# Two-layer decoder on one core: the layer norm's epsilon in the statistics, shorter gate weights, one rounding step, and a new instruction order

## The reference, cut to what matters

```python
def _layernorm(x, axis=-1, eps=1e-05):
    m = jnp.mean(x, axis=axis, keepdims=True)
    v = jnp.var(x, axis=axis, keepdims=True)
    return (x - m) / jnp.sqrt(v + eps)
...
    # _L0_ffn_ref
    a_scale = jnp.max(jnp.abs(x), axis=-1, keepdims=True) + EPS
    z = jnp.clip(x / a_scale * 127.0, -128.0, 127.0)
    a_quant = z + jax.lax.stop_gradient(jnp.round(z) - z)
...
    # _L1_ffn_ref
    gate_logits = jax.nn.softmax(x @ gate_w + gate_b, axis=-1)
    selected = (gate_logits >= THRESHOLD).astype(x.dtype)
    weights = gate_logits * selected
    wsum = jnp.sum(weights, axis=-1, keepdims=True)
    weights = weights / jnp.where(wsum == 0, jnp.ones_like(wsum), wsum)
```

## Time and profile before

| what | value |
|---|---|
| time, median of 3 runs | 508.68 us (508.4 to 509.6) |
| span of the profiled execution | 507.0 us |
| PE busy | 492.5 us, 97% |
| PEld busy | 417.4 us, 82% |
| ACT busy | 438.2 us, 86% |
| DVE busy | 411.2 us, 81% |
| POOL busy | 390.3 us, 77% |
| DMA, mean over the span | 17 GB/s |

### The profile page before, as it was taken

How to read it: one execution, slowest core, us unless ns; L and a number is a source line. 1 busy time by engine, 2 the same in 40 slices (tenths; PEclk the granted TensorE clock), 3 DMA queues, 4 the chain that set the end, 5 groups by cost and what they waited for, 6 DMA issues and landing times.

```text
span 507.0 us, 15965 instructions
## 1 busy us (share of the span) xinstructions
PE 492.5 (97%) x5508; PEld 417.4 (82%) x5508; DVE 411.2 (81%) x939; ACT 438.2 (86%) x1177; POOL 390.3 (77%) x553
## 2 busy tenths in 40 slices
PE   6999999999999999999999999999999999999994
PEld 3878887788888888889888888888988888888882
DVE  3867787887989888989898898888888788876665
ACT  4988889999999888998899998999889899898761
POOL 3787678787678689897798877988777788685663
PEclk8999999999999999999999999999999999999998
DMA  6800000000000000000000000000000000000000
GB/s 197 324 3 2 1 3 1 3 3 2 1 3 1 8 2 8 1 7 3 7 3 7 2 2 8 2 6 3 8 6 2 7 1 5 6 1 8 1 6 16
DMA packets 6462, 8.65 MB, mean 17 GB/s; under 512 B 1393, under 2 KB 4849, under 8 KB 6385
## 3 DMA queue, kind: packets, MB, share of 16 engines
q1 hardware_dynamic: 5952, 6.86, 4.1%
q10 hardware_dynamic: 432, 0.79, 0.5%
HBM read 6.50 MB, written 1.05 MB: 15 GB/s over the span
## 4 chain that ended last, share of the span: by engine, by line
PE 76%; DVE 9%; ACT 6%; issue 3%; DVEq 3%; POOL 1%; DMA 1%; POOLq 0%; SPq 0%; ACTq 0%
PE psum L1188 11%; PE psum L1215 8%; PE psum L1243 8%; PE psum L1175 8%; PE psum L1131 7%; PE psum L1162 5%; ACT w_cross L776 3%; PE psum L1201 2%; PE psum L1360 2%; PE psum L1254 2%; PE psum L1234 2%; PE psum L1226 2%; PE psum L1228 2%; PE psum L1227 2%; PE psum L1236 2%
## 5 line engine op out<-in xcount | busy, mean ns | idle before, releaser
L694 POOL TENSOR_TENSOR w_self<-w_self 128x1024 f16<-128x1024 f32 x64 | 120.9, 1899 | 13.8 <-ACT w_self L759 9.9
L776 ACT ACTIVATE w_cross<-psum,row_max_cross 128x128 f32<-128x128 f32 x384 | 104.5, 405 | 6.8 <-DVE row_max_cross L922 6.2
L699 POOL TENSOR_TENSOR w_cross<-w_cross,e_rec_cross 128x1024 f32<-128x1024 f32 x48 | 91.0, 1899 | 10.3 <-DVE e_rec_cross L931 9.7
L922 DVE TENSOR_REDUCE row_max_cross<-psum 128x8 f32<-128x1024 f32 x48 | 58.0, 1214 | 9.9 <-PE psum L1175 9.5
L929 DVE TENSOR_REDUCE e_sum_cross<-w_cross 128x8 f32<-128x1024 f32 x48 | 58.3, 1215 | 1.8 <-ACT w_cross L776 1.7
L1175 PE MATMUL psum<-kT_cross,qT_cross 64*128 64x128 f32 x768 | 54.2, 283 | 0.0
L1215 PEld LDWEIGHTS psum<-w_cross,v_cross 128*64 128x64 f32 x768 | 41.2, 136 | 15.3 <-issue 13.0
L784 ACT ACTIVATE w_cross<-psum 128x1024 f32<-128x1024 f32 x48 | 50.0, 1048 | 3.2 <-PE psum L1188 3.2
L1215 PE MATMUL psum<-w_cross,v_cross 128*64 128x128 f32 x768 | 51.4, 278 | 0.9 <-ACT w_cross L784 0.6
L1175 PEld LDWEIGHTS psum<-kT_cross,qT_cross 64*128 64x128 f32 x768 | 46.2, 187 | 6.9 <-issue 4.8
L1188 PE MATMUL psum<-ident,w_cross 128*128 128x128 f32 x384 | 49.5, 274 | 0.8 <-POOL w_cross L699 0.8
(11 more groups left out here) (198 smaller groups left out, 1412.5 us busy)
## 6 DMA issues: line engine op xcount, KB each, us to landing
out_dram<-x_all SPq DMA_DIRECT2D x16, 64.0 KB, 1.5
x_all<-in_x SPq DMA_DIRECT2D x1, 768.0 KB, 7.0
cT_all<-in_ctx SPq DMA_DIRECT2D x1, 768.0 KB, 9.0
e_k<-in_e_k SPq DMA_DIRECT2D x1, 512.0 KB, 4.7
e_v<-in_e_v SPq DMA_DIRECT2D x1, 512.0 KB, 5.6
e_q<-in_e_q SPq DMA_DIRECT2D x1, 512.0 KB, 8.9
e_o<-in_e_o SPq DMA_DIRECT2D x1, 512.0 KB, 9.7
m_w<-in_m_w SPq DMA_DIRECT2D x1, 512.0 KB, 9.0
```

What stands on the lines that cost most here:

```text
L694: pool.tensor_tensor(L.w_low[u], L.w[u][:], halves(L.w[u][:]), ALU.subtract)\
L699: pool.tensor_tensor(L.diff[u][:].rearrange("p (h k) -> p h k", h=UNIT), L.e[u][:].rearrange("p (h k) -> p h k", h=UNIT), L.e_rec[:, u, :] ...
L776: last = act.activation(L.e[u][:, P * p:P * (p + 1)], S_[:, P * p:P * (p + 1)], ACT.Exp, bias=L.row_max[:, u, p:p + 1])
L922: dve.tensor_reduce(L.row_max[:, u, :], group(i, turn)[:].rearrange("p (h k) -> p h k", h=UNIT), AX_X, ALU.max, negate=True).then_inc(L.ma ...
```

## The change

- The statistics get a third group of three numbers (count 0, mean 0, sum of squares 128 times epsilon), written once at the start for each of the six stages. The aggregate over nine numbers then gives variance plus epsilon, and the addition on POOL goes.
- `gate_weights` compares the unscaled exponentials with a tenth of their sum, takes the masked product and its sum in one instruction, and divides by that sum. The first reciprocal, one of the two scaled copies and the guard go; a copy of the exponentials to SBUF and a multiplication of one column come.
- `round_units` no longer clips ahead of the rounding.
- The planner's costs for `rs`, `ffn.xTe` and `moe.w` are lowered, and so is its cost of a change of tiling ahead of `pv` in cross attention. The strings of PE, DVE, ACT and POOL are new. SP's is the same.

```diff
-        add(f"{L}.rs", "POOL", 1272, [source], [f"{L}.nm"])
+        add(f"{L}.rs", "POOL", 940, [source], [f"{L}.nm"])
...
-    add("moe.w", "DVE", 1650, ["moe.ex"], ["moe.ml", "moe.gT"])
+    add("moe.w", "DVE", 1240, ["moe.ex"], ["moe.ml", "moe.gT"])
...
 ORDER = dict(
     ACT=(
-        "aGaqaIasaKauaMaGa7a5a5awa5aIa5aRa7a7aVaKaybXbXbXaGaAbZb3a7bZa0b3aIaGaMaVbZbZaRa7aKaCb1b1b1a9bbaMaIbd"
+        "aqaGasaIaKa5aMaua5a5aGa5a7awaIaRa7aKa7aVaybXbZbXaAa7bZb1aGb3bZbZaMaVa0aIaRb1aKb1b1bXa9b3aGbba5a7bdaM"
...
 def switch(name):
     step = name.split(".")[1]
-    return 150 if step in ("xT", "oT", "gT", "t") else 107 if step == "pv" and name[:4] == "self" else 196
+    if step == "pv":
+        return 107 if name[:4] == "self" else 147
+    return 150 if step in ("xT", "oT", "gT", "t") else 196
...
-        self.moments = self.sb("moments", [P, 6])
+        self.moments = self.sb("moments", [P, 9])
         self.mean_var = self.sb("mean_var", [P, 2])
-        self.var_eps = self.sb("var_eps", [P, 1])
...
-                pool.tensor_tensor(L.var_eps[:], L.mean_var[:, 1:2], eps[:], ALU.add)
-                pool.drain()
-                pool.tensor_tensor(L.rstd[:], L.var_eps[:], minus_half[:], ALU.pow)
+                pool.tensor_tensor(L.rstd[:], L.mean_var[:, 1:2], minus_half[:], ALU.pow)
...
-                dve.tensor_scalar(units, units, Q_MAX, -Q_MAX - 1, ALU.min, ALU.max)
+
                 if i:
                     dve.wait_ge(x_full, full(i - 1, "ffn.y"))
-                dve.drain()
...
                 dve.wait_ge(gate_exp, i + 1)
-                dve.reciprocal(g_rec[:], g_sum[:])
-                dve.drain()
-                dve.tensor_scalar(g_soft[:], gates(i, 1), g_rec[:], None, ALU.mult)
-                dve.tensor_scalar(gates(i, 2), gates(i, 1), g_rec[:], None, ALU.mult)
-                dve.drain()
-                dve.scalar_tensor_tensor(out=gates(i, 3), in0=gates(i, 2), scalar=THRESHOLD, in1=g_soft[:],
+                dve.tensor_copy(g_exp[:], gates(i, 1))
+                dve.tensor_scalar(g_least[:], g_sum[:], THRESHOLD, None, ALU.mult)
+                dve.drain()
+                dve.scalar_tensor_tensor(out=gates(i, 2), in0=gates(i, 1), scalar=g_least[:], in1=g_exp[:],
                                          op0=ALU.is_ge, op1=ALU.mult, accum_out=g_keptsum[:])
                 dve.drain()
-                dve.tensor_scalar(g_guarded[:], g_keptsum[:], 0.0, g_keptsum[:], ALU.is_equal, ALU.add)
-                dve.drain()
-                dve.reciprocal(g_rec2[:], g_guarded[:])
+                dve.reciprocal(g_rec[:], g_keptsum[:])
...
+            for L in stages.values():
+                dve.memset(L.moments[:, 6:8], 0.0)
+                dve.memset(L.moments[:, 8:9], P * LN_EPS)
             dve.memset(g_weight[:], 0.0).then_inc(consts, 1)
```

More of the change, by code:

```diff
@@ L80, in norm @@
         fill(f"{L}.xT", 109, [f"{L}.un" if L == "ffn" else f"{L}.nm"], f"{L}.{read}", users)
-        add(f"{L}.xTe", *(("DVE", 572) if L == "ffn" else ("ACT", 332 if L == "moe" else 166)), [f"{L}.xT"])
+        add(f"{L}.xTe", *(("DVE", 250) if L == "ffn" else ("ACT", 332 if L == "moe" else 166)), [f"{L}.xT"])
     def self_attention(L, source, maxima, following, loads, loads_out):
@@ new lines @@
+        "beaUb0b2a4a1a6a4aXaObabWbjbcaLaUblaHaZaQaJa1bebnbWaXbWaLbYaHaOaZbwa4a1a4bab2bcbybjaUbeblbCaQaJbabEbn"
+        "bGbYaXbcbJaZaLb2bja1bebwbla6bya4a6aHbQaObCa6bEbna6baaUbSbGbjbcbUaQbJblb6bebwb8bybnccb0aXaJcabQbCaLbE"
+        "claZbGaHbSa1bUchbjbJcjblb6bwcqb8bacabyccclbncsbQaOa4b2bcbWbCaQbSbEcubUaJchaUbwa6bWbybeb6cqcaaXbJcsaZ"
+        "b8aLbGaHcya1clcccja4cBcCcubjbQb2aObCaJcGblbSa4baaUcya6bcbEbUbncBaQchbeb6bGcCbJaXcacKb8cGcqaLbwclcjcs"
+        "ccbQaZbycubWbSaHa1bYbjbUaOblbaaJbYbcbCaUcybnbEaQcqcBbGbWcKcCchb6bebJcscjbwcab8bycGaXclccaZa4aLa1bQcu"
@@ new lines @@
+        "bjaHa6aObCaJb0blbSbEaQbGbUbncybaaUcqcBcKbcchbJcsbeaXb6cCcaaZbwb8aLa1aHbyclcjccbQcGb2bWcubScKbjbUbCaO"
+        "blbab0bEbncyaQbcaJaUcBcCb6cqb8bGbebJcsaXchbwcaaLaZcccjcGbycla6a1cubjbQaHa4aOblbaaJa4bnaQbSbccybCaUbU"
+        "cKbEcBchcCcqbebJcscjaXb6bWaLb8aHbwaZcaa1bGbyccclcGcubjbYbQaOblbCbSb2bEbUbaaQbccybncKchb6aUcBb8bGcabe"
+        "bJcjbYcqcCccclcsaXcGbwcuaLbybjaJaZbQb0b0a1blaOaHbCbnbSbEa6a6aQbGcyaJbYcKbUcBaUbacCbcchcqb6bwbebJaXca"
+        "b8aLbycGcjcsccaZaHcla1cubjbYb0aOblbQb2bnbaaUbccyaQcKbSchcBaJcqbeaXbUcCcjcsaOb6b0aZb8bCcabEbGaLaQa1cc"
@@ new lines @@
+        "aYcmcda2bRcocvcfaPaTbocAbVcDaEcLcFbubKbNbfaYcIbxbha2cmbzcdbRcocvcLcfbVaPaTcAbocDcFcIbubfbNbKaYbhaEbx"
+        "cdbzcma2cfcvcobRaPaTbocAbVcDcLaEcFcIbubfbNbKaYbhbxa2aEcdbzcmcvcfbRaPbVaTcAcobocDcFcLbfbKbNbhcIbucdcm"
+        "bxaYcvbzcfbRa2coaPboaTcLcAbVcDbucFcIbxbfbNbKaYbhbzcdcma2cvcfcoaTaPbRbocAcDcLcFbfbVaYcIbhaPaTbua2cdbx"
+        "cmbzcfcvaYcobKbNboa2cAcDbfcLcFbhbRcIbubVbNbfcLbKcvbxbhcdbzcmbRcAbocfcDcocFbVcIbobubKbNbxbzcmcdbucvbR"
+        "cfcobxcAbVcDcLcFcIbzbNbKcdcmcvcfbRbKbVcobNcAcDcFcmbRcdbVcocfcLcIcvcdcAcmcLcfcocDcFcvcIcAcDcFcvcLcIcA"
@@ new lines @@
+        "aIaRaKaGaVa0bga5b1a5a9b3a7aCbbbXbkbdaMaVbmaIa0aRaKaGbgbXbtaIaMbZbvbXa0a9a5aGa5bbb3bda9bkbBaVbmbDaRbg"
+        "bbbHbFbZbtbdaKaMbva0bLbkbOb3bga7aIa9a7bBa5bmbDa7bFa7bbbTaVbHbkbdbtaRaGb5bvbmb7bLbOb9bgbBb1cecbbDaKbF"
+        "a0bHbTaMaIcncibtbkb5a9bvckb7bObmb9bbcbbLcrcecnctbtbBb3a5bdbDbXaRbvbTaGbFaKciaVb5a7bXb7crbgcbcxcta0bL"
+        "bHb9czaMbOaIcncka5cEcebkbBb3a9bDcHaKbTcxbmbba5aVcza7bFbdcEaRb5cibtb7bHbgbvaGbLcbb9bOcHcrckctcna0aMce"
+        "bXbTaIbZbkcxa9bBbmbbaKb5bDbZaVczbdbFaRcEaGbXbHcrbtb7cibvbgbOctcbb9cHbLcka0cncea5aMaIbBbka9cxa7bDaKb1"
@@ L545, in decoder @@
         g_rec = sb("g_rec", [P, 1])
-        g_soft = sb("g_soft", [P, EXPERTS])
+        g_exp = sb("g_exp", [P, EXPERTS])
+        g_least = sb("g_least", [P, 1])
         g_keptsum = sb("g_keptsum", [P, 1])
-        g_guarded = sb("g_guarded", [P, 1])
-        g_rec2 = sb("g_rec2", [P, 1])
         g_weight = sb("g_weight", [P, P])
@@ L890, in stats @@
                     dve.wait_ge(L.rstd_ready, i)
-                dve.bn_stats(L.moments[:], x)
+                dve.bn_stats(L.moments[:, 0:6], x)
                 dve.drain()
```

64 lines of the change are left out of this document (22 added, 42 removed).

## The result

The changed kernel takes 504.94 us (median of 5 runs, 504.84 to 506.29); the kernel before took 508.8 beside it (5 runs, 508.4 to 510.17). The ratio is 0.9928, with a 95% interval of 0.991 to 0.9947: faster by 0.7%, 3.9 us. The profiled execution's own time is 504.84, its span 503.1.

A forecast was written before the change was run, and what follows sets the result against it. PE was taken as the bound, its products busy for 97% of the 507.0 us span. Gains of 1.35 (start), 0.87 (end) and 0.7 (ramps), together 2.92, plus 1.68 from span to median gave 505.8 us, range 503.9 to 508.6.

The forecast's parts named there:

- the case of a faster kernel: Whole kernel: a mean below 507.15 us, given a chance of 0.71.
- Part 1: Norms on POOL: 0.34 us less each, 32.6 in all; nothing in the dense middle, full at start and last `moe`.
- The Trainium skill's warning: From 200 to 450 us, PE's busy products hide waits the new order removes: 3.3 us more, 502.5; chance 0.04.
- Part 2: Start: PE's first filler `cross0.k.0(0)` moves from 8.82 to 7.45, a gain of 1.35 us; twelve memsets cost 0.
- the lead of the start is lost: Waits come later, before 50 us, so the start's gain goes: 507.6 us, no change that can be told; chance 0.22.
- the rival with the clock: Below 20 us, PE works without a gap and keeps full clock: about 1.5 us more, 504.3; chance 0.14.
- Part 3: Clip on DVE, dense middle and ramps: some 0.35 us less per sequence, 5.6 in all, taken as worth 0.
- Part 4: Last `moe`: gate weights 0.53 us shorter plus the last norm's 0.34, so 0.87 gained after the last `cross1.y`.
- a sign of being wrong: At the end: a weighing on DVE that waits for POOL's mix of sequence 14 would show the forecast wrong.
- Part 5: Ramps: shorter chains arrive late less often, recovering 0.7 of PE's 3.92 us idle in ramps and middle.
- The rival of new waits: From 200 to 450 us, PE steps stand ahead of their inputs: 510.6 us at 0.3 us per sequence; chance 0.10.

The follow-up runs named there:

- experiment 7: Changed kernel with the old norm statistics (six numbers, addition of epsilon back on POOL): 514.78 us, ratio 1.011 to the kernel before.
- experiment 1: Kernel before with all code edits but its old planner costs and old order: 507.17 us, ratio 0.9955 to the kernel before.
- Experiment 10: Kernel before with seven unneeded PE products at its start and, of the change, only the statistics' third group: 506.81 us, ratio 0.9946.
- experiment 4: Changed kernel with DVE's low part of the context's first four sequences waiting for the first rstd: 506.6 us, ratio 0.9941 to the kernel before.
- experiment 3: Kernel before with seven unneeded PE products at its start, nothing else moved: 507.59 us, ratio 0.9967 to the kernel before.
- experiment 11: Changed kernel with the clip ahead of the rounding again: 506.65 us, ratio 0.9952 to the kernel before.
- experiment 8: Changed kernel with the old gate weights: 509.23 us, ratio 0.9996 to the kernel before.
- experiment 5: Kernel before with all code edits, old planner costs and order, and seven unneeded PE products at its start: 504.98 us, ratio 0.9915.
- experiment 2: Kernel before with the new planner costs and new order but all old code: 520.0 us, ratio 1.0208 to the kernel before.
- experiment 9: Kernel before with seven unneeded PE products at its start and the addition of epsilon done twice in each norm: 522.17 us, ratio 1.025.
- experiment 6: Changed kernel with three unneeded PE products at the start (one warming, two ahead of the first qk): 505.68 us, ratio 0.9929.
- experiment 12: Changed kernel with DVE's low part waiting for the first rstd and three unneeded PE products at the start: 505.59 us, ratio 0.9927.

## Why the prediction was right, step by step

The forecast was 505.8 and the measured time is 504.94, within the range, and the case of a faster kernel came true. Its total is better than its parts, and that is luck: the term of the start failed and another gain stood in its place, the term of the end came out right from two parts that didn't, and the term of the ramps was too small and had the wrong mechanism.

- **Part 1, `rs`.** Right on POOL, and the aggregate over nine numbers costs 14 ns (196 for 182), as taken. At the chain's end it counts only under the new order: from the last `cross1.y` to the logits it is 4.00 us in the changed kernel and 4.32 with the old norm (experiment 7), but 4.49 with and without it under the old order (experiment 1). Wrong was the sentence that it is worth nothing in the dense middle because PE is idle for 0.30 us there. Experiment 10 finds 1.1 us for the norm in the old order, none of it at the end, and experiment 1 a lead that grows by 0.37 us between 193 and 437 us. PE's "busy" time has modelled ends and may cover short waits; no trace shows them singly. The Trainium skill's warning that I quoted among the rivals ("Perfetto Trace Analysis", Identifying the Most-Contended Engine) fits this, though the size was far below the 3.3 us that I had priced.
- **Part 2, the start: the step that failed.** I gave the filler's move 1.35 us. It moved by 0.99, since the low part that the new order put beside the norm made POOL's multiplication 0.55 us longer (experiment 4). And against experiment 3, which has the old filler's time and the full clock, nothing of that lead is left at the first residual or behind it: the rival "the lead of the start is lost" describes what happened to it. What the start did bring was the rival with the clock: 1.5 us (experiment 3), in place of the 1.35. That the two are nearly the same is chance. The twelve memsets were hidden, as taken: DVE still waited 1.18 us for `x`.
- **Part 3, the clip.** Taken at nothing; it is worth 1 to 1.6 us in the new order (experiment 11).
- **Part 4, gate weights, and the end.** Forecast 0.87, measured 0.88 (12.43 for 13.31), but from other parts. Up to the logits it is 0.49 (4.49 to 4.00), not 0.34, and the new order is needed for it: under the old one it is nothing (experiment 1). From the logits to the weighing it is 0.42 (2.95 to 2.53), not 0.53. The gate weights by themselves gave 0.62 (experiment 1), since the copy from PSUM took 0.17 and let the next instruction start after 0.08, less than I took; 0.20 of that was lost again to the wait for POOL's mix of sequence 14. I had named this wait as a sign of being wrong, and had left the residual between gate weights and weighing out of the sum. What I missed is their worth in the middle: with the old ones the new order loses 3.5 us (experiment 8, 2.6 to 3.2 past the start).
- **Part 5, the ramps.** Forecast 0.7 of PE's visible idle time. Visible idle time from 20 to 200 us didn't change (2.35 to 2.33), so the mechanism as I put it is wrong. In its place the code won 1.2 to 1.6 us before the last `cross1.y`: 1.61 in experiment 1 against the kernel before, 1.17 in experiment 5 (489.03) against experiment 3 (490.20), whose first filler had started 0.53 earlier than that of 5.

Measured, then: 0.88 at the end (0.6 from the code, 0.3 from the new order), 1.5 for the clock, and 1.2 to 1.6 for the code on the way. That is 3.6 to 4.0 of the 3.9 us of span; for the new order elsewhere at most 0.3 us is left, which is no more than these readings can be off.

The step from span to time had an error of its own. I took 1.68 us between them, from a span and a median of different executions. In the runs that have both, it is 2.0 to 2.1 us in the kernel before and 1.7 to 1.8 in the changed kernel. So some 0.3 us of the gain lie outside the spans; what they are stays open.

- **The rival of new waits.** It didn't come true, but I had underrated it. I argued that 0.30 us of idle time in 250 "say that the stretch has room". They don't say so. Experiments 2, 7, 8, 9 and 11 show it: 0.34 us more in each norm cost 9.3 us in the new order and 14.4 in the old one, or 0.6 and 0.9 us for each sequence. The new order's losses with single old parts (9.3, 3.5 and 1.2 us) add up to 14.0, near the 14.3 between experiment 2 and the changed kernel.

What stays open: whether the loss comes from the strings themselves or from the PSUM banks, which `Plan` hands out by the modelled costs and which then no longer fit the real times. No kernel here separated the two.

## What to carry to other kernels

Both written-out orders here lose much when their steps get longer. Making steps shorter under the old order was safe and gave 2.3 us. Making the norm longer by 0.34 us cost 9.3 us under the new order and 14.4 under the old one, where 0.34 us less had given about 1.1. The new order was 10.6 us slower without the shorter steps, and with them no faster than the old one that had them and the steady clock. Whether an order that wasn't fitted to its durations would lose less, no kernel here tested. So measure code and order apart before crediting either. Idle time of PE near zero doesn't say that the other engines' savings are worthless, for 1.2 to 1.6 us were won here while it stayed as it was: follow one step of an unchanged order through both traces, and read the lead there, counted from an early event, since starts differ from run to run. Look also at what stands on the engine between two steps of a chain: a residual and a few unneeded products decided here what the shorter norm and gate weights were worth at the end. And look at the first few microseconds at either clock: seven unneeded products in idle places bought 1.5 us and steadier runs.

## What the runs showed of the hardware that I had not expected

- POOL's multiplication of one column took 0.82 us beside DVE's subtraction of two SBUF tensors (5.08 to 5.77), and 0.26 when that came later. It ended 0.14 us after DVE's did. The Trainium skill ("GPSIMD Engine Reference", 2. Architecture) says that GpSimd's physical SBUF ports are shared with DVE; the trace agrees.
- The first load of `x` landed at different times in executions of near kernels: the first statistics started between 3.42 us (experiment 6) and 4.68 (experiment 12).
- The clock granted at the start fell to half for part of the first 20 us after PE had been mostly idle (8.82 to 9.97 for six products in the kernel before), and didn't where unneeded products filled the gaps (experiment 3), nor in the changed kernel. In the window from 0 to 20 us it shows as a mean of 0.91. Where the first products run at half speed without such a fall, the column shows 1.00 (experiments 2 and 12); only the starts of equal products, 0.21 or 0.22 us apart and not 0.11, give it away. So a high mean isn't a fast start: the kernel before had spans of 507.5 to 508.2 in its runs with a mean granted clock of 0.998, and of 506.7 to 507.4 with 0.994.
